# Two decoder layers on one core: the first phase five bodies deep instead of four

## What is computed

```
x = x + mixer(layernorm(x))            # L0: state space mixer, 32 heads of 16, 128 states
x = x + cross_attention(layernorm(x), ctx)   # L0: 16 heads of 16
x = x + experts(layernorm(x))          # L0: 16 experts, the best 2 by softmax, and a shared one

mixer(u): x_ssm, z, B, C, dt = split(u @ in_proj)
          x_ssm = silu(conv4(x_ssm) + b);  dt = softplus(dt + dt_bias);  a = A * dt
          y[t] = sum over s <= t of exp(cum_a[t] - cum_a[s]) * (C[t] . B[s]) * dt[s] * x[s]  + D * x
          out = rmsnorm(y) * silu(z) @ out_proj
```

## Time and profile before

| | us |
|---|---|
| median of 3 runs | 4813.46 (4808.03 to 4820.54) |
| the profiled execution | 4801.35 |
| its span | 4799.7 |
| PE busy | 4216.9 (88%) |
| DVE busy | 3361.2 (70%) |
| ACT busy | 2885.9 (60%) |
| POOL busy | 2721.6 (57%) |

### The profile page before, as it was taken

How to read it: one execution, slowest core, us unless ns; L and a number is a source line. 1 busy time by engine, 2 the same in 40 slices (tenths; PEclk the granted TensorE clock), 3 DMA queues, 4 the chain that set the end, 5 groups by cost and what they waited for, 6 DMA issues and landing times.

```text
span 4799.7 us, 120494 instructions
## 1 busy us (share of the span) xinstructions
PE 4216.9 (88%) x34006; PEld 3007.0 (63%) x34071; DVE 3361.2 (70%) x8668; ACT 2885.9 (60%) x7026; POOL 2721.6 (57%) x4093
## 2 busy tenths in 40 slices
PE   4888888888888888888869979999999999999998
PEld 3555556555655555655647756666666666666665
DVE  3666667667677677677735557777777777777776
ACT  2666666666666666666634436666666666666564
POOL 4666666666666666666622235555555555555554
PEclk7999999999999999999979989999999999999999
DMA  4322222222222222222224411111111111111110
GB/s 129 102 91 81 74 74 74 89 84 74 74 82 91 74 74 82 90 75 74 74 68 147 142 35 32 31 30 29 30 31 31 29 30 31 31 31 31 31 31 19
DMA packets 215885, 304.09 MB, mean 63 GB/s; under 512 B 56608, under 2 KB 167456, under 8 KB 215840
## 3 DMA queue, kind: packets, MB, share of 16 engines
q1 hardware_dynamic: 191376, 249.83, 16.8%
q0 software_dynamic: 19200, 52.45, 3.4%
q10 hardware_dynamic: 5264, 1.25, 0.1%
HBM read 239.19 MB, written 64.23 MB: 63 GB/s over the span
## 4 chain that ended last, share of the span: by engine, by line
PE 57%; DVE 19%; issue 10%; POOL 6%; ACT 4%; DMA 1%; DVEq 1%; ACTq 1%; SPq 1%; POOLq 1%
PE Q L1424 21%; PE Q L1429 10%; PE Q L1417 5%; PE Q L1467 4%; DVE arena L829 4%; DVE arena L827 3%; PE Q L1774 3%; PE Q L1807 3%; PE Q L1626 3%; PE Q L1458 2%; PE Q L1452 2%; DVE arena L857 2%; DVE mx L779 2%; PE Q L1638 2%; POOL arena L637 1%
## 5 line engine op out<-in xcount | busy, mean ns | idle before, releaser
L1429 PE MATMUL Q<-ident,arena 128*128 128x128 f32 x4768 | 806.5, 293 | 173.4 <-ACT arena L1173 69.9
L1429 PEld LDWEIGHTS Q<-ident,arena 128*128 128x128 f32 x4768 | 558.7, 146 | 409.4 <-issue 149.5
L637 POOL TENSOR_TENSOR arena<-arena 128x1024 f32<-128x1024 f32 x256 | 479.6, 1890 | 35.7 <-DMA arena<-cum_rows 35.5
L1424 PE MATMUL Q<-Wkvl,arena 128*128 128x512 f32 x1024 | 499.6, 600 | 0.0
L701 POOL TENSOR_TENSOR l<-l,half_pow 128x8 f32<-128x8 f32 x192 | 318.5, 1659 | 228.5 <-DVE l L1054 226.6
L726 POOL TENSOR_TENSOR arena<-arena,part_of 128x512 f32<-128x512 f32 x256 | 263.7, 1041 | 190.1 <-DVE part_of L1092 189.8
L779 DVE TENSOR_REDUCE mx<-Q 128x4 f32<-128x512 f32 x512 | 343.8, 682 | 10.6 <-PE Q L1452 6.0
L1467 PE MATMUL Q<-arena 128*17 128x128 f32 x4096 | 245.8, 313 | 115.1 <-ACT arena L1190 115.1
L1458 PE MATMUL Q<-ident,arena 128*128 128x128 f32 x2048 | 301.5, 280 | 13.5 <-ACT arena L1190 11.0
L1458 PEld LDWEIGHTS Q<-ident,arena 128*128 128x128 f32 x2048 | 231.3, 142 | 122.8 <-issue 76.1
L1183 ACT ACTIVATE arena<-Q,mx 128x128 f32<-128x128 f32 x1024 | 281.9, 373 | 1.0 <-DVE mx L779 1.0
(11 more groups left out here) (311 smaller groups left out, 10676.5 us busy)
## 6 DMA issues: line engine op xcount, KB each, us to landing
arena<-cum_rows SPq DMA_DIRECT2D x256, 512.0 KB, 6.1
arena<-routed_rows SPq DMA_DIRECT2D x144, 128.0 KB, 2.1
expert_rows<-arena POOLq DMA_DIRECT2D x144, 128.0 KB, 2.0
arena<-in_x_dram SPq DMA_DIRECT2D x128, 128.0 KB, 5.1
arena<-in_ctx_dram SPq DMA_DIRECT2D x128, 128.0 KB, 6.2
x_rows<-arena SPq DMA_DIRECT2D x128, 128.0 KB, 1.7
arena<-x_rows SPq DMA_DIRECT2D x128, 128.0 KB, 2.3
out_dram<-arena SPq DMA_DIRECT2D x64, 128.0 KB, 1.7
```

The costliest lines, as they stand in the source:

```text
L637: tell(g.tensor_tensor(E8[j], E8[j], cums[:, 8 * j:8 * j + 8].unsqueeze(2).broadcast_to([P, 8, T]), ALU.subtract), "diff")
L1424: last = mm(out, lhs(c), rhs(c), start=c == 0, stop=c == n - 1)
L1429: last = nc.tensor.transpose(out[:, c * P:(c + 1) * P], src[:, c * P:(c + 1) * P], ident[:, :])
```

## The change

The norm of the mixer's input becomes a chain of its own, I, on SP, POOL, DVE and ACT, and runs one sequence ahead: a body now runs I for sequence n, M and V for n-1, N for n-2, Y and X for n-3, and F for n-4. There are 68 bodies instead of 67. The order of steps in a body is written anew for all five engines. The matmuls of `awake` are gone. The weights for the later phases come in 21 pieces, one at the end of each of the first 21 bodies, instead of 14 in four bodies; for that SP's first 21 bodies are written out (`apart`), and the other engines loop from the fifth.

```diff
 ORDER = {
     1: {
         "SP": """
-            Ncb0 Ncb1 Ncb2 Yc Xm Mx Ncb3 Nx Mco Fm Fo
+            Ix Ncb0 Ncb1 Ncb2 Yc Xm Ncb3 Nx Mco Fm Fo
         """,
         "POOL": """
-            Nd0 Nd1 Nd2 Xx1r Fln3 Xln2 Mln1 Nd3 Msp Nm3 Fsc Nyg Nrms
+            Nd0 Nd1 Nd2 Nd3 Xx1r Fln3 Xln2 Msp Nm3 Fsc Iln1 Nyg Nrms
         """,
...
-        signals("M", "DVE", "ln1_var dt_pre ratio")
+        signals("I", "DVE", "ln1_var")
+        signals("I", "ACT", "ln1_xn")
+        signals("I", "POOL", "ln1_rstd")
+        signals("M", "DVE", "dt_pre ratio")
...
+            for n in range(depth, apart):
+                body(n, 0, depth - 1)
+                between(n)
+            with eng.Fori(max(depth, apart), NB) as i:
...
-            def M(b):
+            def I(b):
                 yield "x"
                 was(sp, "ln1_xn", b)
                 tell(sp.dma_start(xa, rows(x_d, b)), "xa_in", 16)
+
+            def M(b):
                 yield "co"
...
+                for_, half_ = n // 4, slice(n % 4 // 2 * (NE // 2), (n % 4 // 2 + 1) * (NE // 2))
+                if n < 8:
+                    rows_, cols, src = slice(for_ * P, (for_ + 1) * P), slice(n % 2 * FF, (n % 2 + 1) * FF), (w_g, w_u)[n % 2]
+                    fetched(Wgu[:, half_, for_, cols], src[half_, rows_, :].rearrange("e p f -> p e f"))
...
+            program(sp, "SP", 1, (("I", I, 0), ("M", M, 1), ("N", N, 2), ("Y", Y, 3), ("X", X, 3), ("F", F, 4)), later, 21)
...
+            def I(b):
+                yield "ln1"
+                was(act, "ln1_Tps", b)
+                normal("ln1", xa, xn0, mvM, b)
...
-                done(pe, "dt_pre", b)
-                awake(Q[0][:, 0:2 * T], 5)
...
-                        awake(Q[3][:, :], 5)
```

More of the change, by code:

```diff
@@ L50 @@
         "SP": """
-            Ncb0 Ncb1 Ncb2 Yc Xm Mx Ncb3 Nx Mco Fm Fo
+            Ix Ncb0 Ncb1 Ncb2 Yc Xm Ncb3 Nx Mco Fm Fo
         """,
         "POOL": """
-            Nd0 Nd1 Nd2 Xx1r Fln3 Xln2 Mln1 Nd3 Msp Nm3 Fsc Nyg Nrms
+            Nd0 Nd1 Nd2 Nd3 Xx1r Fln3 Xln2 Msp Nm3 Fsc Iln1 Nyg Nrms
         """,
         "DVE": """
-            Fln3 Xln2 Nm0 Mln1 Fr Yk Ftop Mdt Fslot Msp Xm0 Xm1 Fhg Nm1 Nm2 Xm2 Xm3 Fxo Vcv Vcv1 Vcv2 Vcv3 Ny0 Vxs2 Ny1 Vcb Vxdt Vgz Nx1 Xho
+            Fln3 Xln2 Nm0 Mdt Fr Yk Msp Ftop Fslot Xm0 Xm1 Fhg Nm1 Nm2 Xm2 Xm3 Fxo Vcv Vcv1 Vcv2 Ny0 Ny1 Vcv3 Iln1 Vxs2 Vcb Vxdt Vgz Xho Nx1
         """,
         "ACT": """
-            Ng0 YcT Ne0 Ng1 Fln3 Xln2 Fln3n Xmr Xln2n Mln1 Frx Mln1n Xq Mab Vbc Ne1 Ng2 Yv Fth Ne2 Ng3 FhT Ne3 Xm0 Xm1 Vxp Xm2 Mcum Xm3 NYt0 Xt0 NYt1 Xt1 Vcth Xt2
+            Ng0 YcT Ne0 Ng1 Mln1n Fln3 Xln2 Fln3n Xmr Xln2n Mab Frx Xq Vbc Ne1 Ng2 Yv Fth Ne2 Ng3 FhT Ne3 Xm0 Xm1 Vxp Xm2 Mcum Xm3 NYt0 Xt0 NYt1 Xt1 Vcth Iln1 Xt2
             Xt3 Nsq XOT NyT Vtz
@@ L63 @@
         "PE": """
-            YcT Yk Nv0 Fln3n Yv Xln2n Fr Mln1n Xq Vbc Mdt Frk Xs0 Fgu Fguh Vip1 Vip1h FhT Xs2 Fdn Mcum Nv1 Nv2 Xt0 Nv3 Xt1 Ny0 Xt2 VCB Ny1 Xt3 Xpv Xpv0 VxsT Xpv1
-            Xpv2 NyT Xpv3 Vz Vzh Npr Nprh XOT
+            YcT Mln1n Yk Mdt Nv0 Fln3n Yv Xln2n Fr Xq Vbc Frk Xs0 Fgu Fguh Vip1 Vip1h FhT Xs2 Fdn Mcum Nv1 Nv2 Xt0 Nv3 Xt1 Ny0 Xt2 VCB Ny1 Xt3 Xpv Xpv0 VxsT Xpv1
+            Xpv2 NyT Xpv3 Vz Vzh XOT Npr Nprh
         """,
@@ L276, in two_layers @@
         sig("gathered", 32)
-        signals("M", "DVE", "ln1_var dt_pre ratio")
+        signals("I", "DVE", "ln1_var")
+        signals("I", "ACT", "ln1_xn")
+        signals("I", "POOL", "ln1_rstd")
+        signals("M", "DVE", "dt_pre ratio")
         signals("M", "PE", "ln1_Tps dt cumps")
-        signals("M", "ACT", "ln1_xn ln1_T dt_abs dt_exp cums cumT")
-        signals("M", "POOL", "ln1_rstd a")
+        signals("M", "ACT", "ln1_T dt_abs dt_exp cums cumT")
+        signals("M", "POOL", "a")
         signals("V", "DVE", "conv xs2 cbm xdt gz")
@@ L356, in weave, with program @@
                     steps[n] = 0
-        def program(eng, engine, phase, stages, between=None):
+        def program(eng, engine, phase, stages, between=None, apart=0):
             def body(n, first, last):
@@ new lines, in later @@
+                if n < 8:
+                    rows_, cols, src = slice(for_ * P, (for_ + 1) * P), slice(n % 2 * FF, (n % 2 + 1) * FF), (w_g, w_u)[n % 2]
+                    fetched(Wgu[:, half_, for_, cols], src[half_, rows_, :].rearrange("e p f -> p e f"))
+                elif n < 12:
+                    some = slice(4 * (n - 8), 4 * (n - 7))
+                    fetched(Wd[:, some, :], w_d[some].rearrange("e p d -> p e d"))
+                elif n < 15:
+                    k = n - 12
+                    fetched((Wq1, Wk1, Wv1)[k][:, :, :], w_qkv[:, k * D:(k + 1) * D].rearrange("(c p) n -> p c n", p=P))
+                elif n < 19:
+                    dst, src = ((Wp1, w_proj), (Wql, wq1), (Wkvl, wkv1), (Wol, wo1))[n - 15]
+                    fetched(dst[:, :, :], src.rearrange("(c p) n -> p c n", p=P))
+                elif n < 21:
+                    fetched(lno[:, n - 19, :], (lno_w, lno_b)[n - 19].partition_broadcast(P))
@@ L489, in _ @@
+            counts["w_later"] = 16 * 21
+            program(sp, "SP", 1, (("I", I, 0), ("M", M, 1), ("N", N, 2), ("Y", Y, 3), ("X", X, 3), ("F", F, 4)), later, 21)
             for other in ("PE", "DVE", "ACT", "POOL"):
@@ L604, in centre @@
                 tell(g.tensor_tensor(mv[:, 5:6], mv[:, 4:5], mv[:, 3:4], ALU.mult), f"{n}_rstd")
+            def I(b):
+                yield "ln1"
+                centre("ln1", mvM, b, "I_POOL")
             def M(b):
-                yield "ln1"
-                centre("ln1", mvM, b, "M_POOL")
                 yield "sp"
@@ L666, in F @@
                          "scattered", 16)
-            program(pool, "POOL", 1, (("M", M, 0), ("N", N, 1), ("X", X, 2), ("F", F, 3)))
+            program(pool, "POOL", 1, (("I", I, 0), ("M", M, 1), ("N", N, 2), ("X", X, 3), ("F", F, 4)))
             met(pool, "POOL", 1)
@@ L799, in _, with I @@
             wide = lambda t: t.unsqueeze(2).broadcast_to([P, NH, HP])
+            def I(b):
+                yield "ln1"
+                done(dve, "xa_in", b, 16)
+                moments("ln1", xa, stM, mvM, "I_DVE", b)
             def M(b):
                 J = lambda ins, bare=False: link(dve, "M_DVE", b, ins, bare)
-                yield "ln1"
-                done(dve, "xa_in", b, 16)
-                moments("ln1", xa, stM, mvM, "M_DVE", b)
                 yield "dt"
@@ L1190, in evac, with I @@
                     tell(s_.activation(PT[:, j, :, :], cut(banks[j][:, :], NG), ACT.Copy), f"PT{n}s")
+            def I(b):
+                yield "ln1"
+                was(act, "ln1_Tps", b)
+                normal("ln1", xa, xn0, mvM, b)
             def M(b):
-                yield "ln1"
-                normal("ln1", xa, xn0, mvM, b)
                 yield "ln1n"
@@ L1430, in transposes, with lnT @@
                 return last
[L1432 to L1438, removed]
+            def lnT(n, src, bank, b):
                 done(pe, f"{n}_xn", b)
```

19 lines of the change are left out of this document (4 added, 15 removed).

## The result

| | before | after |
|---|---|---|
| median | 4810.74 us, 4 runs (4805.82 to 4820.54) | 5211.46 us, 4 runs (5202.33 to 5214.88) |
| ratio to before | | 1.0837, 95% interval 1.0821 to 1.0853 |
| span of the profiled execution | 4799.7 us | 5213.3 us |
| mean granted clock of PE | 0.947 | 0.893 |

The change makes the kernel slower by 401 us. The prediction said slower, by the same chain of waits, and 5100: 290 us. The time lies 11 us outside its range.

What follows compares the result with a forecast made beforehand. Bound: a ring of waits per sequence, 37.5 us a body. With 29.1 + 13.2 = 42.3, plus 0.2, 60 bodies take 42.5 each; +301 less 8 on 4801.35 gives 5094, taken as 5100 us; range 4930 to 5200.

Steps and rivals of the forecast that it cites:

- The second part, SP held at `Ix`: SP's load of x waits for ACT's norm, holding four reads and POOL's Nd: 13.2 us from norm to next L654.
- The first part, ACT's wait: ACT's norm, ahead of Xt2, waits for moments and scale: done 3.0 us after the convolution's end.
- the way through PE: From the norm's end through ACT's copies and PE to x1: 10.2 us, 3.0 us to spare against the DMA way.
- its stretch at half clock: PE at 1.2 GHz from L1467 to x1 costs 1.5 us, lengthening that way to 11.7 us at most.
- So L946 comes 0.2 us later: Front of the body: softplus adds about 0.7 us ahead of L946, L604's vanished wait returns 0.5 us.
- the cold front: Rival, chance 0.05: half clock for most of the body, router and scores 3 us longer, body 45.5, 5274 us.
- the 0.5 us that L604 was to give back: POOL's L604 waits during DVE's L857; that wait falls away when L654 starts after L857: 0.5 us.
- the 26.1 us to the end of the convolution: L654 to the convolution's end: 25.9 us before, 26.1 us after, so the front of the ring gives nothing.
- The ends: First x1 about 8 us sooner; second sequence's body 38 us; the last two bodies 37.5 and 36 us.
- The unread products cost nothing before, as they stood in idle time: The removed PE matmuls had cost no time before; the skill's activity rule speaks against removing them.
- The port rule: DVE and GpSimd block each other on shared ports; 0.2 us put, 43.5 us body if all L857 conflicts.
- Rival 1: SP is not held, only ACT's wait counts: body 39.4 to 40.9, 4908 to 5002 us, chance 0.10.

Runs made afterwards that it cites:

- e1: The changed kernel with SP loading x for the norm behind its reads of the cumulated sums, not ahead of them: 4984.34 us, ratio to before 1.0362.
- e2: The changed kernel with ACT applying the norm behind the copies Xt2, Xt3 and the square, not ahead of them: 5199.92 us, ratio to before 1.0815.
- e4: The changed kernel with the two groups of unread matmuls put back where they were: 5191.0 us, ratio to before 1.0783.
- e10: The changed kernel with DVE's three softplus operations back behind the slots, not ahead of the choice of experts: 5205.68 us, ratio to before 1.0811.
- e9: The kernel before without its two groups of unread matmuls: 4817.74 us, ratio to before 1.0004.
- e7: e6 with the two groups of unread matmuls put back: 4936.95 us, ratio to before 1.0254.
- e6: The changed kernel with the load late, the whole norm early in the body's front, and POOL's fourth Nd back behind the norms' scales: 4916.79 us, ratio 1.0217.

## Why the prediction was right, and where it failed

**The second part, SP held at `Ix`: right.** All of its signs are in the trace, and e1 shows that they are the cost. From the tanh's start to L664 the sum was 3.0 + 13.2 = 16.2 us; the bodies took 16.58. Its terms in the body shown: norm done 3.2 us after the tanh's start (3.0), then 0.9 to the first read's issue (0.8), 5.15 to POOL's start (4.9), 7.6 for the four `Nd` (7.5).

**The first part, ACT's wait: right in size, and rightly beside the path.** 3.2 us after the tanh's start; e2 shows that it alone is worth 12 us or nothing while SP is held. The sum gave the way through PE 3.0 us to spare, and 1.5 with its stretch at half clock. In the body shown x1 was 3.2 us early, on average 1.6 (x1 15.0 us after the tanh, L664 16.6).

**"So L946 comes 0.2 us later": the step that failed.** The sum for L664 to L958 was 6.7 us. The bodies took 8.6. That is 1.9 us more in each, and the 60 bodies for which the text had 42.5 us took 44.4, 1.9 more as well. The front can be cut in three: from L664 to ACT's norm for the router (L1185 with mvF, before L1173), from there to DVE's first read of the router's product (L954, before L942), with PE's transposes and products between them, and from there to L958. Means over the bodies from 930 us:

| | clock in the front | to L1185 | to L954 | to L958 | sum |
|---|---|---|---|---|---|
| before | 1.00 | 2.84 | 2.82 | 0.80 | 6.47 |
| after | 0.68 | 3.11 | 4.13 | 1.36 | 8.60 |
| e4, 20 bodies | 1.00 | 3.11 | 2.83 | 1.36 | 7.30 |
| e4, the other 19 | 0.66 | 3.11 | 4.01 | 1.36 | 8.48 |
| e1, 28 bodies | 1.00 | 2.68 | 2.83 | 1.36 | 6.87 |
| e10 | 0.73 | 3.11 | 4.08 | 0.71 | 7.90 |

The middle is PE's clock: 1.3 us, for which the sum had nothing. e4 shows it by itself, with the same orders and full clock in half of its bodies. The text had looked for the clock at the end of the body only, and the cold front was a rival at 0.05 (its way was right, 3 us its size and too much). The first third holds the 0.5 us that L604 was to give back, and it cost 0.3 more instead: DVE's L869 and POOL's L664 start together, L869 takes 1.79 us instead of 1.23 (at 1220.09 in the body shown), and L609 behind L664 takes 1.17 where 0.19 is usual. The last third is the softplus ahead of the choice, 0.6 us, and e10 takes all of it back; the text had 0.7 for it.

```profile
1220.09 1.79 DVE L869 TENSOR_TENSOR arena<-arena 128x1024 f32<-128x1024 f32 x1
```

Against the sum the front so lost 1.3 by the clock and 0.8 by the meeting of L664 and L869, and the softplus cost 0.1 less. In e1, at full clock and with L664 ahead of L869, it takes 6.87 us, near the 6.7 of the sum. Why PE is at its lower level in the front of the changed kernel is known only so far: the unread matmuls bring the clock back in half of the bodies (e4), and the late load in 28 of 40 (e1).

**The rest of the 26.1 us to the end of the convolution: it held.** L958 to the tanh took 19.74 us on average; the sum had 26.1 - 6.7 = 19.4.

**The ends: right in part.** 8 us sooner at the start; the trace has 7. The first interval, for which the text had 38 us, took 45.1; no run tells why. The last two took 70.6 where it had 73.5.

**"The unread products cost nothing before, as they stood in idle time": right for the time of the kernel before.** e9 moves it by 0.04%, inside its interval. But three pairs of traces tell that they keep up the front's clock: with and without them it is full in 39 and 18 of 39 bodies (before, e9), in 20 of 39 and none of 38 (e4, after), and in all 40 and 28 of 40 (e7, e6). The time followed only once, by 20 us in e4. The Trainium skill's rule (TensorE: Matmul & The Clock Gate, section on the HAM clock gate), that activity releases the throttle, agrees with these counts.

**The port rule** of the Trainium skill (SBUF — State Buffer, section on the two sides of SBUF) agrees with e6 and e10, and it weighs more than the 0.2 us given to it: DVE's quarter of the convolution takes 2.14 instead of 1.13 us beside a POOL operation of 1.29.

**Rival 1's upper time** was summed wrong: 1.6 us in 60 bodies off 5094 is 4998, not 5002. The forecast does not rest on it.

**The range** reached to 44.1 us per body as its upper edge, from the landing time and a collision, and took nothing for half clock in the front. The intervals came out at 44.1 on average over the phase, at that edge. The lower part of the stated range, 4930 to 5000, was there for a rival.

## What to carry to other kernels

When an order is written by hand, ask of every wait at the head of an in-order queue what stands behind it: a load of 128 KB that nobody missed held four reads that everybody waited for. Two waits on parallel ways round a ring do not add, so take away the one that ends last, then measure the other. An operation moved into idle time of its own engine can still cost, by the port of a neighbour or by the clock of an engine that now idles longer; sum those two for every part of the ring, not for the part that was edited.

## What was not expected of the hardware

SP issues faster from written-out bodies than from the loop. In the changed kernel, written out, the first read follows the load by 0.44 us:

```profile
507.32 0.34 SPq L430 DMA_DIRECT2D arena<-in_x_dram  x1
507.76 1.33 SPq L444 DMA_DIRECT2D arena<-cum_rows  x3
```

In the loop it is 0.73 us (1252.21 to 1252.94), and so in every body from 851 us on. Where SP's issue is on the path, this shows: in the 13 bodies between 320 and 930 us, nearly all of them written out, POOL's first `Nd` starts 8.1 us after the tanh and a body takes 43.2 us; in the 38 between 930 and 2700 us it is 9.0 and 44.9. That the loop's code is the cause of all of this difference was not tested by itself.
